# Second norm by halves, convolution edge columns from PSUM, weight splits and constants re-spread over the engines

## The chip, the cores and the metric

One core of one Trainium2 chip. The metric is the device time of one execution in microseconds (us), the median of three runs. Engines, by the names of the profile: PE (TensorE matmuls; PEld its weight loads), DVE (VectorE), ACT (ScalarE), POOL (GpSimd), SP (SyncE, which issues nearly all DMAs).

## The reference

x is (2, 512, 256): two sequences of 512 tokens. xn is its layernorm over the last axis. The output is x + attn(xn) + ffn(xn).

```
y    = gelu(xn @ w_y + b_y)
xb   = xn @ w_x + b_x
conv = conv_b + sum over k of conv_w[k] * xp[:, k:k+T]     # 4 taps, xp is xb with 3 zeros ahead
gx, ga = sigmoid(conv @ w_ig + b_ig), sigmoid(conv @ w_ag + b_ag)
a    = exp(-8 * ga * softplus(a_param));  h = scan of a, gx * conv * sqrt(1 - a*a)
attn = (h * y) @ w_out + b_out
ffn  = (silu(xn @ q(w1).T) * (xn @ q(w3).T)) @ q(w2).T      # q: ternary, threshold mean(|w|) / 2
```

## The kernel before

Tokens lie on partitions for the norm, features for all the rest. A sequence is four tiles of 128 tokens, and 256 features are two chunks. Each engine has one list of instructions in an order written out by hand, and semaphores join the lists; an engine that waits holds up everything behind it in its own list.

Products with the dense weights run in a rounded type. For accuracy each operand is split: `hi` is the rounded copy, `lo` is the value less `hi`. A product is then three terms (hi by hi, w_lo by hi, w_hi by lo), which for one sequence are 12 matmuls of 512 columns.

The order of work around the change, before:

- SP loads four tiles of x of sequence 0 one by one, w_x, the whole of sequence 1 in one DMA (L188), then w_y, w_ig, w_ag, w1, w3, w2, w_out, b_out.
- DVE sets constants, among them two stretches of padding in `gt` (L431, L432), takes statistics (L436, L441) and adds eps (L444); POOL raises the variance to -0.5 (`rstd_of`, L231); DVE normalises (L449). Sequence 0 goes by halves of two tiles, sequence 1 as one piece of four.
- PE transposes xn (L636). ACT rounds the transposed halves from PSUM (`xt_hi_of`, L288); DVE takes the rest (`xt_lo_of`, L455). DVE's list has the statistics of sequence 1, which wait for its load, ahead of `xt_lo_of(0)`.
- PE makes xb of sequence 0 by halves (`first_x_terms`, L740: hi by hi, w_lo by hi, w_hi by lo), then y of sequence 0 (L647), with the transposes of sequence 1 in the middle of it, then xb and y of sequence 1, then the gates, the sum of |w1| and |w3| by a product with ones (L727), and the hidden layer (`hidden`, L664), `down` (L696) and `project` (L706).
- The rounded dense weights `w_hi` of w_x, w_y, w_ig and w_ag are made by ACT (`square_hi`, L283), their `w_lo` by POOL (`square_lo`, L226), each matrix in one instruction.
- The bias b_x passes through the convolution. POOL makes tap constants in `conv_constants` (L233 to L247), the sum of all four in `conv_c` and corrections for the first three columns in `head`. ACT writes the newest tap with that sum (`newest_tap`, L317); DVE adds `head` to the first three columns (L488) and then the three older taps (L492).
- ACT rounds conv (L342) and POOL takes the rest (`lo_of_conv`, L251). DVE makes the ternary w1 and w3 (`ternary_13`, L468, L471).
- ACT loads the table of gelu where gelu first comes (L324). The rounded b_out (`b_split`, L398 on ACT, L272 on POOL) is made before the hidden layer.
- PE begins with 12 matmuls on ones (`warm`, L713), and one more behind each of two waits (L717 to L720).

Of the kernel before, what the change touches and what calls it, by code (L numbers as in the profile page):

```python
# [19 lines left out]
P = 128  # L20
SEQS, SEQ = 2, 512
# [22 lines left out]
def build(nc: bass.Bass, x, dense, w13t, w2t, params, b_out, out):  # L44
# [7 lines left out]
    with ctx:  # L52
# [46 lines left out]
        head = sb("head", [P, TAPS - 1, KC])  # L99
        conv_c = sb("conv_c", [P, 2, KC])  # L100
# [37 lines left out]
        x_loaded = [sem(f"x_loaded{i}") for i in range(TILES + 1)]  # L138
# [13 lines left out]
        b_tap_set, head_set, conv_c_set = sem("b_tap_set"), sem("head_set"), sem("conv_c_set")  # L152
# [28 lines left out]
        def _(sp):  # L181
# [6 lines left out]
            sp.dma_start(x_sb[:, 1], x_dram[1]).then_inc(x_loaded[TILES], 16)  # L188
# [24 lines left out]
        def _(pool):  # L213
# [10 lines left out]
            def square_lo(m):  # L224
                pool.wait_ge(w_hi_set, m + 1)
                nc.gpsimd.tensor_tensor(w_lo[:, m], w_raw[:, m], w_hi[:, m].bitcast(f32), ALU.subtract).then_inc(w_lo_set, 1)  # L226
# [6 lines left out]
            def conv_constants():  # L233

                b_x = par[:, B_X:B_X + KC]
                pool.wait_ge(par_loaded, 16)
                for k in range(TAPS):
                    nc.gpsimd.tensor_tensor(b_tap[:, k], par[:, CONV_W + KC * k:CONV_W + KC * (k + 1)], b_x, ALU.mult).then_inc(b_tap_set, 1)
                pool.wait_ge(b_tap_set, TAPS)
                nc.gpsimd.tensor_scalar(head[:, TAPS - 2], b_tap[:, 0], -1.0, None, ALU.mult).then_inc(head_set, 1)  # L240
                nc.gpsimd.tensor_tensor(conv_c[:, 0], b_tap[:, TAPS - 1], par[:, CONV_B:CONV_B + KC], ALU.add).then_inc(conv_c_set, 1)
                for k in range(1, TAPS - 1):
                    pool.wait_ge(head_set, k)
                    nc.gpsimd.tensor_tensor(head[:, TAPS - 2 - k], head[:, TAPS - 1 - k], b_tap[:, k], ALU.subtract).then_inc(head_set, 1)
                pool.wait_ge(head_set, TAPS - 1)
                pool.wait_ge(conv_c_set, 1)
                nc.gpsimd.tensor_tensor(conv_c[:, 1], conv_c[:, 0], head[:, 0], ALU.subtract).then_inc(conv_c_set, 1)  # L247
# [20 lines left out]
            for s in range(SEQS):  # L268
                for c in range(KC):
                    lo_of_conv(s, c)  # L270
            pool.wait_ge(b_hi_set, 1)
            nc.gpsimd.tensor_tensor(b_split[:, 1], b_row[:, :], b_split[:, 0].bitcast(f32), ALU.subtract).then_inc(b_split_set, 1)  # L272
            for n in range(2 * FULL):
                lo_of_g(n)


        @block.scalar
        def _(act):
# [32 lines left out]
            def newest_tap(s):  # L311

                act.wait_ge(conv_c_set, 2)
                act.wait_ge(xb_psum, s + 1)
                k = TAPS - 1
                for c in range(KC):
                    nc.scalar.activation(conv[:, s, c], slot[X_SLOT[s]][:, c], ACT.Identity,  # L317
                                         scale=par[:, CONV_W + KC * k + c:CONV_W + KC * k + c + 1],
                                         bias=conv_c[:, 1, c:c + 1]).then_inc(tap_set, 1)
# [38 lines left out]
            def decays(s):  # L358

                act.wait_ge(rate_set, 2)  # L360
# [12 lines left out]
            xt_hi_of(0)  # L373
            square_hi(WY)
            newest_tap(0)
            square_hi(WIG)
# [3 lines left out]
            square_hi(WAG)  # L380
            conv_hi_of(0, 0)
            act.wait_ge(w3_loaded, 16)
            abs_sum_of(w13_raw[:, :, W3_AT:W13], KC, junk_b, 1, abs13_set)
            newest_tap(1)
# [12 lines left out]
            act.wait_ge(b_out_loaded, 16)  # L397
            nc.scalar.activation(b_split[:, 0], b_row[:, :], ACT.Copy).then_inc(b_hi_set, 1)  # L398
# [3 lines left out]
            act.wait_ge(w_lo_set, WIG + 1)  # L402
# [25 lines left out]
        def _(dve):  # L428
            nc.vector.memset(quarter[:, :], 0.25).then_inc(quarter_set, 1)
            nc.vector.memset(mult[:, :, :, 0:1], 0.5).then_inc(mult0_set, 1)  # L430
            nc.vector.memset(gt[32:HALF].bitcast(f32), 1.0).then_inc(gt_pads_set, 1)  # L431
            nc.vector.memset(gt[96:P].bitcast(f32), 0.0).then_inc(gt_pads_set, 1)  # L432
# [5 lines left out]
            def variance(s, tiles):  # L438
# [43 lines left out]

            def older_taps(s, c):

                dve.wait_ge(tap_set, KC * s + c + 1)
                dve.wait_ge(head_set, TAPS - 1)
                step = (TAPS - 1) * (KC * s + c)
                nc.vector.tensor_tensor(conv[:, s, c, 0:TAPS - 1], conv[:, s, c, 0:TAPS - 1], head[:, :, c], ALU.add).then_inc(tap_step, 1)  # L488
# [100 lines left out]
            dve.wait_ge(sp_log, 1)  # L589
            nc.vector.scalar_tensor_tensor(out=sp_e[:, 1], in0=par[:, A_PARAM:A_PARAM + KC], scalar=0.0, in1=sp_e[:, 2],  # L590
                                           op0=ALU.max, op1=ALU.add).then_inc(rate_set, 1)
            dve.wait_ge(rate_set, 1)
            nc.vector.tensor_scalar(a_rate[:, :], sp_e[:, 1], -4.0, None, ALU.mult).then_inc(rate_set, 1)
            older_taps(0, 0)
            xt_lo_of(1)
            older_taps(0, 1)
            older_taps(1, 0)
            older_taps(1, 1)
# [31 lines left out]
        def _(pe):  # L630
            def transposes(s):

                for t in range(TILES):
# [7 lines left out]
            def dense_terms(dst, m, terms, first, last, chunk_ready=None):  # L641
                for c in range(KC):
# [68 lines left out]
            def warm(count):  # L711
                for _ in range(count):
                    nc.tensor.matmul(slot[WARM_SLOT][:, 0, 0:P], ones[:, :], ones[:, :], start=True, stop=True)  # L713

            pe.wait_ge(ones_set, 1)
            warm(WARM)
            pe.wait_ge(mv_set, TILES)  # L717
            warm(1)
            pe.wait_ge(rstd_set, 1)
            warm(1)  # L720
            pe.wait_ge(ident_set, 1)
            transposes(0)
# [11 lines left out]
            def first_x_terms(weights, part, ready):  # L734
                for h in range(2):
                    pe.wait_ge(ready, h + 1)
                    for c in range(KC):
                        for o in range(KC):
                            for w in weights:
                                mm = nc.tensor.matmul(slot[X_SLOT[0]][:, o, halves[h]], w[:, WX, c, o * P:(o + 1) * P],  # L740
                                                      part[:, 0, c, halves[h]],
                                                      start=(part is xt_hi and h == 0 and c == 0 and w is w_hi),
                                                      stop=(part is xt_lo and c == KC - 1), skip_group_check=True)
# [12 lines left out]
            dense_terms(slot[Y_SLOT[0]], WY, [(w_hi, xt_lo[:, 0])], False, True).then_inc(y_psum, 1)  # L756
# [14 lines left out]
            def gate_product(s, m, slots, done, between=None):  # L771
                pe.wait_ge(w_lo_set, m + 1)
# [6 lines left out]
            pe.wait_ge(w_lo_set, WAG + 1)  # L779
# [65 lines left out]
```

## Time and profile before

| | us |
|---|---|
| runs (3) | 75.23, 75.66, 76.0: median 75.66 |
| the profiled execution, its own time | 75.99 |
| its span, first to last instruction | 74.2 |
| PE busy | 69.2 (93%) |
| DVE, ACT, POOL busy | 61.2, 48.3, 31.5 |

Times in the trace are counted from the span's start. A row of the timeline is a start, a length, the engine, the line of the code, the operation, what it writes and reads, its shape and a count; the length of a row with a count above one runs from the first start to the last end. Idle time just before a row, and what ended it, stands in square brackets.

### The profile page before, as it was taken

The numbers are of one execution on the slowest core, as the hardware profiler recorded it, in microseconds if no ns is written. First come the engines' busy times: TensorE is split into PE (matmuls) and PEld (weight loads), VectorE is DVE, ScalarE is ACT, GpSimd is POOL, SyncE is SP. The second block draws the span as 40 slices with busy tenths as digits, with TensorE's granted clock in tenths as the row PEclk, the third lists the DMA queues.
The fourth block names the chain that finished last, engine by engine and source line by source line (L and its number), as shares of the span: only waits on it lengthen the run. The fifth ranks groups of instructions, "written<-read, shape, count | busy, mean of one in ns | idle before, by whom it ended". The sixth has DMA issues, their size and how long they took to land.

```text
span 74.2 us, 1064 instructions
## 1 busy us (share of the span) xinstructions
PE 69.2 (93%) x364; PEld 58.6 (79%) x364; DVE 61.2 (82%) x101; ACT 48.3 (65%) x75; POOL 31.5 (43%) x43
## 2 busy tenths in 40 slices
PE   4999969999999999999999999999999999999920
PEld 4985758877888888888888888888899999988800
DVE  4897499999999999999979974697960799999750
ACT  3674523899999999999998978466699910000000
POOL 6385647245851680016002979947689000000000
PEclk9999999999999999999999999999999999999999
DMA  0889999920000000000000000000000000000195
GB/s 8 236 289 333 368 379 342 379 97 9 0 0 0 4 0 0 0 0 0 4 1 0 0 9 0 0 0 0 0 0 0 0 0 0 9 0 0 61 322 183
DMA packets 5095, 5.63 MB, mean 76 GB/s; under 512 B 525, under 2 KB 4578, under 8 KB 5090
## 3 DMA queue, kind: packets, MB, share of 16 engines
q1 hardware_dynamic: 4946, 5.55, 22.1%
q8 instruction: 3, 0.05, 0.3%
q10 hardware_dynamic: 144, 0.01, 0.1%
q14 instruction: 2, 0.02, 0.1%
HBM read 4.51 MB, written 1.05 MB: 75 GB/s over the span
## 4 chain that ended last, share of the span: by engine, by line
PE 80%; DMA 7%; DVE 5%; SPq 3%; issue 1%; DVEq 0%
PE slot L664 25%; PE slot L647 23%; PE slot L696 14%; PE slot L706 8%; DMA x_sb<-x 7%; PE slot L767 4%; PE slot L673 2%; SPq L186 2%; DVE stats L436 2%; PE slot L740 2%; DVE x_sb L551 1%; PE slot L636 1%; DVE xt_lo L455 1%; SPq L183 1%; DVEq L52 0%
## 5 line engine op out<-in xcount | busy, mean ns | idle before, releaser
L256 POOL TENSOR_TENSOR g_lo<-w_raw,g_hi 128x512 fp32r<-128x512 f32 x10 | 14.1, 1421 | 9.0 <-ACT g_hi L338 8.9
L664 PE MATMUL slot<-xt_hi,w_q 128*128 128x512 f32 x40 | 15.7, 393 | 0.0
L664 PE MATMUL slot<-xt_lo,w_q 128*128 128x512 f32 x40 | 15.7, 393 | 0.0
L514 DVE SCALAR_TENSOR_TENSOR w_raw<-w_raw,s,slot 128x512 f32<-128x512 f32 x10 | 7.3, 747 | 3.1 <-ACT w_raw L332 3.0
L696 PE MATMUL slot<-w_q,g_hi 128*128 128x256 f32 x40 | 9.7, 283 | 0.0
L696 PE MATMUL slot<-w_q,g_lo 128*128 128x256 f32 x40 | 9.7, 283 | 0.0
L492 DVE SCALAR_TENSOR_TENSOR conv<-slot,par,conv 128x511 f32<-128x511 f32 (+2 forms) x12 | 9.0, 748 | 0.4
L664 PEld LDWEIGHTS slot<-xt_hi,w_q 128*128 128x128 f32 x40 | 7.5, 188 | 1.7
L664 PEld LDWEIGHTS slot<-xt_lo,w_q 128*128 128x128 f32 x40 | 7.5, 188 | 1.7
L332 ACT ACTIVATE w_raw<-slot,scale 128x512 f32<-128x512 f32 x10 | 6.6, 684 | 3.1 <-PE slot L664 3.1
L696 PEld LDWEIGHTS slot<-w_q,g_lo 128*128 128x128 f32 x40 | 7.7, 192 | 0.0
L696 PEld LDWEIGHTS slot<-w_q,g_hi 128*128 128x128 f32 x40 | 7.7, 192 | 0.0
L226 POOL TENSOR_TENSOR w_lo<-w_raw,w_hi 128x512 fp32r<-128x512 f32 x4 | 5.2, 1295 | 4.5 <-ACT w_hi L283 3.7
L706 PE MATMUL slot<-w_raw,tx 128*128 128x256 f32 x32 | 7.1, 379 | 0.0
L338 ACT ACTIVATE g_hi<-w_raw 128x512 fp32r<-128x512 f32 x10 | 6.3, 629 | 1.1 <-DVE w_raw L514 0.9
L251 POOL TENSOR_TENSOR conv_lo<-conv,conv_hi 128x512 fp32r<-128x512 f32 x4 | 5.4, 1354 | 3.3 <-ACT conv_hi L342 3.3
L706 PEld LDWEIGHTS slot<-w_raw,tx 128*128 128x128 f32 x32 | 6.0, 190 | 0.8
L713 PE MATMUL slot<-ones 128*128 128x128 f32 x28 | 5.3, 357 | 1.0 <-POOL ones L214 1.0
L713 PEld LDWEIGHTS slot<-ones 128*128 128x128 f32 x28 | 4.8, 261 | 1.4 <-POOL ones L214 1.0
L533 DVE TENSOR_TENSOR tx<-tx,mult 128x512 f32<-128x512 f32 x4 | 2.7, 685 | 2.8 <-ACT mult L370 2.8
L538 DVE TENSOR_TENSOR_SCAN tx<-ta,tx 128x512 f32<-128x512 f32 x4 | 4.9, 1224 | 0.1
L647 PE MATMUL slot<-conv_hi,w_hi 128*128 128x512 f32 x12 | 4.7, 395 | 0.0
(111 smaller groups left out, 144.5 us busy)
## 6 DMA issues: line engine op xcount, KB each, us to landing
w_raw<-w13t SPq DMA_DIRECT2D x2, 682.0 KB, 7.6
w_raw<-dense SPq DMA_DIRECT2D x5, 256.0 KB, 5.6
out<-x_sb SPq DMA_DIRECT2D x3, 256.0 KB, 2.2
w_raw<-w2t SPq DMA_DIRECT2D x1, 640.0 KB
x_sb<-x SPq DMA_DIRECT2D x4, 128.0 KB, 2.3
x_sb<-x SPq DMA_DIRECT2D x1, 512.0 KB, 5.3
out<-x_sb SPq DMA_DIRECT2D x2, 128.0 KB, 2.1
w_raw<-w2t SPq DMA_DIRECT2D x2, 42.0 KB
```

The lines of the kernel that those rows point to most:

```text
L226: nc.gpsimd.tensor_tensor(w_lo[:, m], w_raw[:, m], w_hi[:, m].bitcast(f32), ALU.subtract).then_inc(w_lo_set, 1)
L251: nc.gpsimd.tensor_tensor(conv_lo[:, s, c], conv[:, s, c], conv_hi[:, s, c].bitcast(f32), ALU.subtract).then_inc(conv_lo_set, 1)
L256: nc.gpsimd.tensor_tensor(g_lo[:, j, s], g[:, n % RING], g_hi[:, j, s].bitcast(f32), ALU.subtract).then_inc(g_lo_set, 1)
L332: nc.scalar.activation(silu[:, n % RING], slot[H_SLOT[s][j]][:, 0], ACT.Silu, scale=scale[:, 0:1]).then_inc(silu_set, 1)
L338: nc.scalar.activation(g_hi[:, j, s], g[:, n % RING], ACT.Copy).then_inc(g_hi_set, 1)
L492: nc.vector.scalar_tensor_tensor(out=conv[:, s, c, i:], in0=slot[X_SLOT[s]][:, c, 0:SEQ - i], scalar=par[:, CONV_W + KC * k + c:CONV_W + K ...
L514: nc.vector.scalar_tensor_tensor(out=g[:, n % RING], in0=silu[:, n % RING], scalar=s32[:, 0:1], in1=slot[H_SLOT[s][j]][:, 1], op0=ALU.mult ...
L647: mm = nc.tensor.matmul(dst[:, o], w[:, m, c, o * P:(o + 1) * P], v[:, c], start=(first and i == 0 and c == 0), stop=(last and i == len(te ...
L664: mm = nc.tensor.matmul(slot[H_SLOT[s][j]][:, o], w13_q[:, c, col:col + P], v[:, s, c], start=(c == 0 and v is xt_hi), stop=(c == KC - 1 a ...
L696: nc.tensor.matmul(out_tile(s, i, t), v[:, s, rows], w2_q[:, j], start=(j == 0 and t == tiles.start and k == 0), stop=False, skip_group_ch ...
L706: mm = nc.tensor.matmul(out_tile(s, i, t), tx[:, s, c, t * P:(t + 1) * P], w_raw[:, WOUT, c], start=False, stop=(c == KC - 1), skip_group_ ...
L713: nc.tensor.matmul(slot[WARM_SLOT][:, 0, 0:P], ones[:, :], ones[:, :], start=True, stop=True)
```

## The change

- Sequence 1 is loaded by two DMAs and goes through statistics and norm by halves. `xt_lo_of(0)` comes ahead of its statistics.
- Adding eps moves from DVE to POOL, in `rstd_of`. `tap_sum(1..3)` come behind the two `rstd_of` of sequence 0.
- PE: in xb of sequence 0 the lo term of the first half comes ahead of the second half's hi term, and the w_lo terms come third. In y of sequence 0 the w_lo term comes last, behind the transposes of sequence 1, and by chunks. Two single `warm` matmuls go; one of 64 columns comes between the halves of the first transposes.
- `head` goes: `conv_c[k]` is the sum of the first k + 1 constants, ACT writes columns 3 and up, and DVE writes columns 0 to 2 from PSUM (`first_columns`), for the first chunk of sequence 0 between the two halves of the second norm.
- POOL: `w_lo` of w_y waits until all of xn is made and is done in two chunks; `w_hi` of w_ig and w_ag move from ACT to POOL; the decay rates and the padding of `gt` move from DVE to POOL, between the four `lo_of_conv`; `b_split` moves (on ACT and POOL) behind the fifth hidden block.
- ACT: one gelu of one column, on a zero that DVE sets, comes ahead of `square_hi(WY)`, so that gelu's table is loaded there. `gate_x(0)` comes ahead of `conv_hi_of(1, 1)`, the sum of |w3| ahead of `conv_hi_of(0, 0)`.

```diff
             square(WX)
-            sp.dma_start(x_sb[:, 1], x_dram[1]).then_inc(x_loaded[TILES], 16)
+            for i in range(2):
+                t = slice(i * TILES // 2, (i + 1) * TILES // 2)
+                sp.dma_start(x_sb[:, 1, t], x_dram[1][:, t]).then_inc(x_loaded[TILES + i], 16)
...
+            def square_hi(m):
+                pool.wait_ge(w_loaded[m], 16)
+                nc.gpsimd.tensor_copy(w_hi[:, m], w_raw[:, m]).then_inc(w_hi_set, 1)
...
             def rstd_of(s, tiles, ready):
+                pool.wait_ge(mv_set, TILES * s + tiles.stop)
+                nc.gpsimd.tensor_scalar(v_eps[:, s, tiles], mv[:, s, tiles, 1], EPS, None, ALU.add).then_inc(v_set, 1)
                 pool.wait_ge(v_set, ready)
...
-            conv_constants()
-            nc.gpsimd.tensor_scalar(half_b[:, :], par[:, B_IG:B_IG + 2 * KC], 0.5, None, ALU.mult).then_inc(half_b_set, 1)
+            tap_biases()
+            tap_sum(0)
             rstd_of(0, slice(0, TILES // 2), 1)
             rstd_of(0, slice(TILES // 2, TILES), 2)
+            for i in range(1, TAPS):
+                tap_sum(i)
             pool.wait_ge(xn_set, TILES)
             square_lo(WX)
-            rstd_of(1, slice(0, TILES), 3)
-            square_lo(WY)
-            square_lo(WIG)
-            square_lo(WAG)
...
+            rstd_of(1, slice(0, TILES // 2), 3)
+            rstd_of(1, slice(TILES // 2, TILES), 4)
+            pool.wait_ge(xn_set, 2 * TILES)
+            for c in range(KC):
+                square_lo(WY, range(c, c + 1))
+            for m in (WIG, WAG):
+                square_hi(m)
+                square_lo(m)
+            lo_of_conv(0, 0)
+            half_biases()
+            rates()
+            lo_of_conv(0, 1)
+            gt_pads(slice(32, HALF), 1.0, KC)
...
+            lo_of_conv(1, 0)
+            gt_pads(slice(96, P), 0.0, KC + 1)
...
+            lo_of_conv(1, 1)
...
             xt_hi_of(0)
+            act.wait_ge(quarter_set, 2)
+            nc.scalar.activation(gelu_in[:, 1:2], gelu_in[:, 0:1], ACT.Gelu)
             square_hi(WY)
             newest_tap(0)
-            square_hi(WIG)
             xt_hi_of(1)
...
+            def first_columns(s, c):
...
+                nc.vector.scalar_tensor_tensor(
+                    out=conv[:, s, c, 0:k], in0=slot[X_SLOT[s]][:, c, 0:k],
+                    scalar=par[:, CONV_W + KC * k + c:CONV_W + KC * k + c + 1],
+                    in1=conv_c[:, 0:k, c], op0=ALU.mult, op1=ALU.add).then_inc(tap_step, 1)
...
-            dve.wait_ge(x_loaded[TILES], 16)
-            statistics(1, range(TILES))
-            variance(1, range(TILES))
             xt_lo_of(0)
-            normalise(1, range(TILES), 3)
...
+            for i in range(2):
+                dve.wait_ge(x_loaded[TILES + i], 16)
+                statistics(1, tile_halves[i])
+                variance(1, tile_halves[i])
+            normalise(1, tile_halves[0], 3)
+            first_columns(0, 0)
+            normalise(1, tile_halves[1], 4)
             older_taps(0, 0)
             xt_lo_of(1)
...
-            first_x_terms((w_hi,), xt_hi, xt_hi_set)
-            pe.wait_ge(w_lo_set, WX + 1)
-            first_x_terms((w_lo,), xt_hi, xt_hi_set)
-            first_x_terms((w_hi,), xt_lo, xt_lo_set).then_inc(xb_psum, 1)
+            first_x_terms((w_hi,), xt_hi, xt_hi_set, 0)
+            first_x_terms((w_hi,), xt_lo, xt_lo_set, 0)
+            first_x_terms((w_hi,), xt_hi, xt_hi_set, 1)
+            pe.wait_ge(w_lo_set, KC * (WX + 1))
+            for h in range(2):
+                first_x_terms((w_lo,), xt_hi, xt_hi_set, h)
+            first_x_terms((w_hi,), xt_lo, xt_lo_set, 1).then_inc(xb_psum, 1)
             pe.wait_ge(w_hi_set, WY + 1)
-            dense_terms(slot[Y_SLOT[0]], WY, [(w_hi, xt_hi[:, 0])], True, False)
-            pe.wait_ge(w_lo_set, WY + 1)
-            dense_terms(slot[Y_SLOT[0]], WY, [(w_lo, xt_hi[:, 0])], False, False)
-            transposes(1)
-            dense_terms(slot[Y_SLOT[0]], WY, [(w_hi, xt_lo[:, 0])], False, True).then_inc(y_psum, 1)
+            dense_terms(slot[Y_SLOT[0]], WY, [(w_hi, xt_hi[:, 0]), (w_hi, xt_lo[:, 0])], True, False)
+            transposes(1, first_half)
+            transposes(1, second_half)
+            pe.wait_ge(w_lo_set, KC * WY + 1)
+            dense_terms(slot[Y_SLOT[0]], WY, [(w_lo, xt_hi[:, 0])], False, True, chunks=[0])
+            pe.wait_ge(w_lo_set, KC * WY + 2)
+            dense_terms(slot[Y_SLOT[0]], WY, [(w_lo, xt_hi[:, 0])], False, True, chunks=[1]).then_inc(y_psum, 1)
             pe.wait_ge(xt_hi_set, 4)
```

## Rows read from the trace of the kernel before

**Rows 1.** The page: busy time by engine, and the chain that ended last.

```profile
PE 69.2 (93%) x364; PEld 58.6 (79%) x364; DVE 61.2 (82%) x101; ACT 48.3 (65%) x75; POOL 31.5 (43%) x43
...
PE 80%; DMA 7%; DVE 5%; SPq 3%; issue 1%; DVEq 0%
```

**Rows 2.** The chain in order of time: start us, us, what.

```profile
3.04 5.30 DMA x_sb<-x
...
70.17 1.02 DVE x_sb L551 x2
```

**Rows 3.** Timeline of PE, 10.9 to 33.1 us.

```profile
10.90 1.34 PE L740 MATMUL slot<-xt_lo,w_hi 128*128 128x256 f32 x8 [0.63 <-DVE xt_lo L455]
...
13.91 1.04 PE L636 MATMUL slot<-ident,xn_y 128*128 128x128 f32 x8
...
15.71 0.47 PE L647 MATMUL slot<-xt_hi,w_hi 128*128 128x512 f32 x1
16.02 0.39 PE L647 MATMUL slot<-xt_hi,w_lo 128*128 128x512 f32 x1
...
17.68 1.20 PE L647 MATMUL slot<-xt_lo,w_hi 128*128 128x512 f32 x4
...
33.05 0.39 PE L664 MATMUL slot<-xt_hi,w_q 128*128 128x512 f32 x1
```

**Rows 4.** Timeline of DVE, 3 to 32 us.

```profile
3.28 0.75 DVE L436 BATCH_NORM_STATS2 stats<-x_sb 128x6 f32<-128x256 f32 x2
...
5.02 0.30 DVE L441 BATCH_NORM_AGGREGATE mv<-stats 128x2 f32<-128x6 f32 x2
...
5.86 1.54 DVE L449 TENSOR_SCALAR xn_y<-x_sb,mv,rstd 128x256 f32<-128x256 f32 x4 [0.34 <-POOL rstd L231]
...
10.17 1.28 DVE L455 TENSOR_TENSOR xt_lo<-slot,xt_hi 128x512 fp32r<-128x512 f32 x2
...
11.38 1.37 DVE L449 TENSOR_SCALAR xn_y<-x_sb,mv,rstd 128x256 f32<-128x256 f32 x1
...
13.91 0.16 DVE L488 TENSOR_TENSOR conv<-conv,head 128x3 f32<-128x3 f32 x1
14.11 2.32 DVE L492 SCALAR_TENSOR_TENSOR conv<-slot,par,conv 128x511 f32<-128x511 f32 x3
...
25.11 3.16 DVE L468 TENSOR_SCALAR below<-w_raw,thr 128x1408 bf16<-128x1408 f32 x2
28.19 3.22 DVE L471 SCALAR_TENSOR_TENSOR w_q<-w_raw,thr,below 128x1408 fp32r<-128x1408 f32 x2
```

**Rows 5.** Timeline of POOL.

```profile
0.86 0.20 POOL L215 MEMSET ident<- 128x128 f32 x1
...
1.07 0.31 POOL L217 MEMSET w_raw<- 128x256 f32 x1
...
4.91 0.22 POOL L259 TENSOR_SCALAR half_b<-par 128x4 f32<-128x4 f32 x1
5.09 1.53 POOL L231 TENSOR_TENSOR rstd<-v_eps,power 128x2 f32<-128x2 f32 x2
...
11.31 1.29 POOL L226 TENSOR_TENSOR w_lo<-w_raw,w_hi 128x512 fp32r<-128x512 f32 x1
...
33.09 1.45 POOL L272 TENSOR_TENSOR b_split<-b_row,b_split 1x256 fp32r<-1x256 f32 x1 [5.55 <-ACT b_split L398]
...
49.31 1.29 POOL L256 TENSOR_TENSOR g_lo<-w_raw,g_hi 128x512 fp32r<-128x512 f32 x1 [1.16 <-ACT g_hi L338]
```

**Rows 6.** Timeline of ACT, 7 to 24 us.

```profile
7.93 0.60 ACT L288 ACTIVATE xt_hi<-slot 128x512 fp32r<-128x512 f32 x1 [0.21 <-PE slot L636]
...
9.08 0.63 ACT L283 ACTIVATE w_hi<-w_raw 128x512 fp32r<-128x512 f32 x1 [0.55 <-DMA w_raw<-dense]
...
21.19 1.28 ACT L324 ACT_TABLE_LOAD   x1
22.48 1.27 ACT L324 ACTIVATE xn_y<-slot,par 128x512 f32<-128x512 f32 x2
```

More of the change, by code:

```diff
@@ L98, in build @@
         b_tap = sb("b_tap", [P, TAPS, KC])
-        head = sb("head", [P, TAPS - 1, KC])
-        conv_c = sb("conv_c", [P, 2, KC])
+        conv_c = sb("conv_c", [P, TAPS, KC])
+        gelu_in = sb("gelu_in", [P, 2])
         abs_sum = sb("abs_sum", [P, 4])
@@ L135, in xt_bank @@
             return slot[T_SLOT[s]][:, h].rearrange("p (c n) -> p c n", c=KC)
-        x_loaded = [sem(f"x_loaded{i}") for i in range(TILES + 1)]
+        x_loaded = [sem(f"x_loaded{i}") for i in range(TILES + 2)]
         w_loaded = [sem(f"w_loaded{m}") for m in range(5)]
@@ L316, in newest_tap @@
                 for c in range(KC):
-                    nc.scalar.activation(conv[:, s, c], slot[X_SLOT[s]][:, c], ACT.Identity,
+                    nc.scalar.activation(conv[:, s, c, k:], slot[X_SLOT[s]][:, c, k:], ACT.Identity,
                                          scale=par[:, CONV_W + KC * k + c:CONV_W + KC * k + c + 1],
-                                         bias=conv_c[:, 1, c:c + 1]).then_inc(tap_set, 1)
+                                         bias=conv_c[:, k, c:c + 1]).then_inc(tap_set, 1)
             def gelu_of(s):
@@ L416, in _ @@
             g_hi_of(4)
+            act.wait_ge(b_out_loaded, 16)
+            nc.scalar.activation(b_split[:, 0], b_row[:, :], ACT.Copy).then_inc(b_hi_set, 1)
             for n in range(FULL, 2 * FULL):
@@ L583, in _ @@
                 normalise(0, tile_halves[i], i + 1)
-            dve.wait_ge(x_loaded[TILES], 16)
-            statistics(1, range(TILES))
-            variance(1, range(TILES))
             xt_lo_of(0)
-            normalise(1, range(TILES), 3)
[L589 to L593, printed above, removed]
+            for i in range(2):
[5 more added lines that the diff above has]
+            normalise(1, tile_halves[1], 4)
             older_taps(0, 0)
             xt_lo_of(1)
+            first_columns(0, 1)
             older_taps(0, 1)
-            older_taps(1, 0)
-            older_taps(1, 1)
+            for c in range(KC):
+                first_columns(1, c)
+                older_taps(1, c)
             threshold_13()
@@ L630, in _, with transposes @@
         def _(pe):
-            def transposes(s):
-                for t in range(TILES):
+            def transposes(s, tiles):
+                for t in tiles:
                     pe.wait_ge(xn_set, TILES * s + t + 1)
@@ L639, in transposes, with dense_terms @@
                         mm.then_inc(xt_psum, 1)
-            def dense_terms(dst, m, terms, first, last, chunk_ready=None):
-                for c in range(KC):
+            def dense_terms(dst, m, terms, first, last, chunk_ready=None, chunks=range(KC)):
+                for c in chunks:
                     if chunk_ready:
@@ L709, in project, with warm @@
                             mm.then_inc(o_psum, 1)
-            def warm(count):
+            def warm(count, cols):
                 for _ in range(count):
-                    nc.tensor.matmul(slot[WARM_SLOT][:, 0, 0:P], ones[:, :], ones[:, :], start=True, stop=True)
+                    nc.tensor.matmul(slot[WARM_SLOT][:, 0, 0:cols], ones[:, :], ones[:, 0:cols], start=True, stop=True)
+            first_half, second_half = range(0, TILES // 2), range(TILES // 2, TILES)
             pe.wait_ge(ones_set, 1)
[L716 to L720, printed above, removed]
+            warm(WARM, P)
             pe.wait_ge(ident_set, 1)
-            transposes(0)
+            transposes(0, first_half)
+            warm(1, P // 2)
+            transposes(0, second_half)
             def sums_of_w13():
@@ L732, in sum_of_w2, with first_x_terms @@
                 nc.tensor.matmul(sum2, ones[:, :], abs_sum[:, 2:4], start=True, stop=True).then_inc(sum2_psum, 1)
[L734 to L743, printed above, removed]
+            def first_x_terms(weights, part, ready, h):
+                pe.wait_ge(ready, h + 1)
+                for c in range(KC):
+                    for o in range(KC):
+                        for w in weights:
+                            mm = nc.tensor.matmul(slot[X_SLOT[0]][:, o, halves[h]], w[:, WX, c, o * P:(o + 1) * P],
+                                                  part[:, 0, c, halves[h]],
+                                                  start=(part is xt_hi and h == 0 and c == 0 and w is w_hi),
+                                                  stop=(part is xt_lo and h == 1 and c == KC - 1), skip_group_check=True)
```

76 lines of the change are left out of this document (39 added, 37 removed).

## The prediction

> **What bounds the kernel now.** I read the page's busy times first: PE is busy for 69.2 of 74.2 us, and the chain that ended last is PE for 80% [rows 1]. So the next question is where PE is not at full pace, and the chain in order of time answers it: PE carries the chain from 10.90 to 70.17, where the last output begins [rows 2, 3]. Behind that point nothing can be won but by fewer or faster matmuls, and the change takes away none there. Ahead of it stands the load of sequence 1 (3.04 to 8.35) [rows 2], and PE idles 0.63 us until the first `xt_lo` of sequence 0 [rows 3]. The timelines of DVE, POOL and ACT then show why it was late: DVE's list puts the statistics of sequence 1 ahead of it, so `xt_lo` began at 10.17 [rows 4] though its `xt_hi` was done at 8.53 [rows 6].
>
> PE's pace is the yardstick for all that follows. From 15.71 (xb of sequence 1) to 33.05 (hidden layer) it does 72 matmuls of 512 columns and two small sums in 17.34 us [rows 3], which is 0.237 each if the two sums together count as one more. There are restarts in it: the first matmul behind a wait holds its successor off 0.31 us instead of 0.23 [rows 3]. I ask when PE reaches xb of sequence 1, and carry the gain from there to the end, wait by wait.
>
> **The change, step by step.**
>
> *First norm.* Statistics of tiles 2 and 3 ended with the second pair of aggregates at 5.32 [rows 4]; one eps instruction of some 0.1 us leaves DVE ahead of them, so 5.2. POOL now adds eps (0.22, as its row of that kind [rows 5]) and raises to the power (1.53 for two, so about 0.8 [rows 5]): 5.2 + 0.1 + 0.25 + 0.8 = 6.4. Two normalisations at 0.4 each, overlapping a little (1.54 for four [rows 4]), end at 7.15, against 7.40. The first half gains more (POOL came to it only at 5.09, behind ten small constants [rows 5]), but the second half sets what follows.
>
> *`xt_lo` of sequence 0.* In the kernel before, `xt_hi` of the second half was done at 8.53, that is 1.13 us behind the last xn [rows 4, 6]. 7.15 + 1.13 = 8.28, and one `xt_lo` (1.28 for two that overlap, so 0.68) gives 9.02 instead of 11.45. PE's xb of sequence 0 then ends near 10.3 instead of 12.1: by 9.0 it has done the first half's hi and lo terms and the second's hi term, has eight w_lo matmuls under way to about 9.9, and four lo matmuls remain.
>
> *Gelu's table.* A load takes 1.28 us [rows 6]. From 8.2, when ACT is done with `xt_hi`, load, gelu of one column (0.2 as a small operation) and `square_hi(WY)` (0.63) end at 10.33. Before, w_y landed at 9.08 [rows 6]. So `square_hi(WY)` is 0.6 late, but PE is ready for it only at 10.3: the cost is 0.1, and even that is covered, since the next thing PE needs comes later still. Nothing is won at the old place either: gelu's results were not what PE waited for.
>
> *Second norm: here the time is set.* DVE is free at 8.94, behind `xt_lo`; the first half of x has to be there by then, the second by 9.8. The whole landed at 8.35 before [rows 2], and the split costs SP one issue more, about 0.45 us. Four statistics at 0.33 and two pairs of aggregates (a pair of both kinds takes 0.97 [rows 4]) end at 10.75. The first half's aggregates are there at 9.9; POOL's eps and power take it to 11.0; the second half's, queued behind, to 12.0. Two normalisations end at 12.8, against 13.72: before, the first of the four took 1.37 us [rows 4] because it met POOL's `w_lo` of w_y (11.31 to 12.60 [rows 5]). A normalisation can be held up by POOL, then, and the first half's pair now starts just as POOL's power of the second half runs. The rows say that a power does not do it: in the first norm the second power (up to 6.62 [rows 5]) ran beside normalisations that took 1.54 for four [rows 4]. I take no loss.
>
> The Trainium skill speaks against the change here (SBUF — State Buffer, Who interferes with whom): a DVE instruction of this mode and any POOL instruction exclude each other for its whole length, whichever begins first. The trace agrees for the subtraction (1.37 for 0.4 [rows 4]) and not for the power. By the rule the first pair would wait for 12.0 instead of 11.1, xn would end at 13.5, and the gain would be 0.35.
>
> `first_columns` (0.16, as the `head` add that it replaces [rows 4]) lies in DVE's wait from 11.8 to 12.0 and costs nothing; without that cover it would cost 0.2.
>
> *w_lo of w_y.* It now waits for the last xn: 12.85, and half of 1.29 with its start is 0.68 [rows 5], so 13.55 and 14.2. PE has done eight hi matmuls of y by 12.3 and eight transposes (0.11 each [rows 3]) by 13.1, waits 0.45, does two matmuls, waits 0.2, does two more, and comes to xb of sequence 1 at 14.75 to 14.9, since two restarts cost 0.1 each. Before: 15.71. **Gain 0.8 to 0.95.**
>
> *From there to the hidden layer.* The restarts at 15.71 and 17.68 go away if `xt_hi` and `xt_lo` of sequence 1 are early: `xt_hi` is done at 14.1, and `xt_lo`, behind older taps of 2.32 us [rows 4] from 12.7, at 16.2, needed at 16.6. The eight matmuls from 15.71 took 1.97 [rows 3] where 1.85 is the pace: **0.1 to 0.2 more.**
>
> POOL's new work is the one unknown. `w_hi` of two matrices comes to it, an operation that the trace shows on no POOL row. Below it stands a bare write: memsets of 128 and 256 columns took 0.20 and 0.31 [rows 5], so 512 would take 0.52. Above it stands the subtraction with two reads, 1.29 [rows 5]. I take 0.9, in the middle, as it has one read. From 14.2: twice (0.9 + 1.29 + waits of 0.1) is 18.75, `lo_of_conv(0, 0)` 20.05, one bias and three rates at 0.25 21.0, `lo_of_conv(0, 1)` 22.3. PE needs this last one at about 22.7 (14.85, 24 matmuls of sequence 1, 8 of the gate, 2 more). Spare: 0.4. At 0.52 it is 1.2; at 1.29 PE waits 0.4.
>
> *Off the path.* Padding on POOL is two memsets of about 0.95 each (0.31 and six times 0.107); they lie between `lo_of_conv`s that PE needs at 27.5, with a us to spare. ACT's two `square_hi` leave it, and `b_split` (0.4 on ACT, 1.45 on POOL [rows 5]) moves into a place where POOL idled 1.16 before its next `g_lo` [rows 5]; its DMA is needed only at the end of `down`. The ternary w1 and w3 ended at 31.41 [rows 4], 1.6 ahead of PE. DVE ends its taps near 23.6, 1.3 earlier than before, so they should end by 30.1 at the old pace, still 1.8 ahead of PE's 31.95; of that the two memsets, now beside the two compares (3.16 [rows 4], with two `lo_of_conv` beside them), could take 1.9 if they held them up fully, so this cover is thin but enough to within 0.1.
>
> **The sum.** 0.85 + 0.2 = 1.05 us. The output and the scan shift with the hidden layer, as no wait between is touched. The profiled execution took 75.99; it becomes 74.9. The median of the runs stands 0.33 below that, so it goes from 75.66 to **74.6**.
>
> **Rivals.**
>
> *The second norm is late (within 1%).* The chain through POOL's two powers and the second half of x decides. If the second half lands at 10.4 instead of under 9.8, or the first pair of normalisations is held behind the second power (0.7 late), 0.6 to 0.7 goes one to one: gain 0.4, 75.3. For it: the one load took 5.30 us [rows 2], and every later load is issued later. Against: 1.4 us of slack on the landing, and the first norm's four at full pace beside a power. The rule of the Trainium skill above is this rival's second condition.
>
> *POOL's list becomes the bound (slower).* Place: `lo_of_conv(0, 1)`, for which PE waits in the first gate. Both copies count, so lateness is twice (copy less 0.9) less the spare 0.4, and the gain is gone at a copy of about 1.6; at 2.2 PE waits 2.2 us and the time is 75.66 - 1.05 + 2.2 = 76.8. For it: POOL's power took 0.8 us for two columns [rows 5], so columns alone don't price an operation there. Against: a subtraction with twice the reads took 1.29.
>
> *The table load costs more in its new place (within 1%).* If it also held ACT back for as long again, about 1.35 us, `square_hi(WY)` would end at 11.7, y of sequence 0 would end near 15.5, and the gain falls to 0.4: 75.3. Against: gelu began 0.01 us behind the load's end [rows 6]. The Trainium skill (ScalarE: Activation LUTs, What ACT_TABLE_LOAD costs) gives a load with its drain as 2.66 us; the trace shows 1.28 alone.
>
> That the table is not kept, and loaded again at the first real gelu, costs the forecast nothing, as the load was not on the path at either place.
>
> **How the numbers follow.** Within 1% (0.76 us) of 75.66 is about what a measurement can tell from no change. The forecast (gain 0.8 to 1.5, the upper end if PE's wait for w_lo of w_y is missing) has 0.72, all of it faster by over 1%. The late second norm has 0.17 and the load's drain 0.03: 0.20 within 1%. POOL's list has 0.08, slower. The range goes from 73.9 (gain 1.5, and 0.25 for a lower draw of the runs) to 75.7: it takes in the second rival and a copy of 1.29, and leaves out the slow copy.
>
> **What would show it.** Right: `xt_lo` of sequence 0 ends near 9.0; normalisations of the second norm at 0.4 each, the last one near 12.8; PE idle 0.4 and 0.2 ahead of the two chunks of w_lo, xb of sequence 1 at 14.8, no idle of PE in the gates, hidden layer at 32.0, span 73.1. Wrong: PE idle ahead of the first gate's lo term (POOL), `square_hi(WY)` ending behind 10.5 (table), statistics of sequence 1 waiting for a load behind 9.0 (DMA).

## The result, and the profile after

The change made the kernel slower: 75.88 us (median of 20 runs, 75.45 to 76.22) against 75.41 (20 runs of the kernel before beside them, 74.89 to 76.6). The ratio is 1.0066, with an interval from 1.0043 to 1.009, which is 0.3 to 0.7 us; the forecast was 74.6. Ratios and intervals, here and below, leave out the slow executions that some kernels had (the slowest, 237.25 us, was the profiled one of `d1_w_lo_early`), so they differ a little from the quotients of the medians, which are of all runs. The profiled execution took 75.86 with a span of 74.0. The page answers to [rows 1]:

```profile
PE 68.6 (93%) x362; PEld 58.7 (79%) x362; DVE 59.0 (80%) x95; ACT 47.7 (64%) x74; POOL 37.4 (51%) x55
...
PE 65%; POOL 12%; DVE 7%; issue 5%; DMA 3%; ACT 2%; DVEq 0%; POOLq 0%
```

PE has only 65% of the chain, against 80%. The chain in order of time [rows 2] tells where it left PE:

```profile
13.79 9.68 PE slot L689 x40
...
37.81 5.55 PE slot L706 x24
...
43.39 0.69 ACT w_raw L371
44.07 0.53 ACT g_hi L377
...
44.67 2.55 POOL g_lo L281 x2
47.22 0.61 DVE gt_hi L608
...
48.49 1.23 DVE gt L609
...
50.24 0.76 DVE w_raw L556
...
51.05 2.11 PE slot L706 x8
```

Before, PE carried the chain from 10.90 to the last output. Now it leaves PE at 43.36, in the middle of the hidden layer, goes through ACT, POOL and two casts of DVE, and is back on PE at 51.05. The timeline of PE, which answers to [rows 3], has both halves of the story:

```profile
10.53 0.50 PE L689 MATMUL slot<-xt_hi,w_hi 128*128 128x512 f32 x1
...
13.79 1.42 PE L689 MATMUL slot<-xt_hi,w_lo 128*128 128x512 f32 x4 [0.27 <-POOL w_lo L233]
15.05 0.40 PE L689 MATMUL slot<-xt_hi,w_hi 128*128 128x512 f32 x1
...
32.11 0.39 PE L706 MATMUL slot<-xt_hi,w_q 128*128 128x512 f32 x1
...
50.34 0.39 PE L706 MATMUL slot<-xt_lo,w_q 128*128 128x512 f32 x1
51.05 0.50 PE L706 MATMUL slot<-xt_hi,w_q 128*128 128x512 f32 x1 [0.31 <-DVE w_raw L556]
```

The front half did what was forecast: the hidden layer begins at 32.11 instead of 33.05 [rows 3]. Its tenth full block of eight matmuls, at 51.05, follows the matmul before it by 0.71 where the pace is 0.23: 0.48 is lost there. DVE and POOL show the same stretch; first DVE, which answers to [rows 4] in its first two lines (the others have no row there):

```profile
11.17 0.73 DVE L484 TENSOR_SCALAR xn_y<-x_sb,mv,rstd 128x256 f32<-128x256 f32 x2 [0.28 <-POOL rstd L249]
12.18 0.74 DVE L484 TENSOR_SCALAR xn_y<-x_sb,mv,rstd 128x256 f32<-128x256 f32 x2
...
47.21 1.24 DVE L608 CAST gt_hi<-w_raw 42x1024 fp32r<-42x1024 f32 x1
48.49 1.72 DVE L609 CAST gt<-w_raw 42x1024 fp32r<-42x1024 f32 x1
50.24 1.41 DVE L556 SCALAR_TENSOR_TENSOR w_raw<-w_raw,s,slot 128x512 f32<-128x512 f32 x2
...
57.73 0.69 DVE L575 TENSOR_TENSOR tx<-tx,mult 128x512 f32<-128x512 f32 x1 [2.83 <-ACT mult L409]
```

Then POOL, which answers to [rows 5]:

```profile
11.41 0.73 POOL L249 TENSOR_TENSOR rstd<-v_eps,power 128x2 f32<-128x2 f32 x1
13.00 1.43 POOL L233 TENSOR_TENSOR w_lo<-w_raw,w_hi 128x256 fp32r<-128x256 f32 x2 [0.86 <-DVE xn_y L484]
14.38 0.61 POOL L228 CAST w_hi<-w_raw 128x512 fp32r<-128x512 f32 x1
...
47.17 0.73 POOL L313 TENSOR_TENSOR b_split<-b_row,b_split 1x256 fp32r<-1x256 f32 x1
48.37 1.30 POOL L281 TENSOR_TENSOR g_lo<-w_raw,g_hi 128x512 fp32r<-128x512 f32 x1 [0.47 <-ACT g_hi L377]
```

And the same two casts in the timeline of DVE of the kernel before:

```profile
47.85 0.85 DVE L566 CAST gt_hi<-w_raw 42x1024 fp32r<-42x1024 f32 x1
48.74 0.69 DVE L567 CAST gt<-w_raw 42x1024 fp32r<-42x1024 f32 x1
49.46 0.75 DVE L514 SCALAR_TENSOR_TENSOR w_raw<-w_raw,s,slot 128x512 f32<-128x512 f32 x1
```

A cast takes 0.69. After the change `b_split` on POOL (47.17 to 47.90) began 0.04 ahead of the first cast, which ended 0.55 behind it, at 48.45. So the second cast started late, at 48.49, when the next `g_lo` had begun (48.37 to 49.67); it ended 0.55 behind that, at 50.21. Two casts of 0.69 became 1.24 and 1.72. The product g behind them, for which PE's tenth block waits, came at 50.24, where before it came at 49.46 although the hidden layer had begun 0.94 later.

My theory from here: the whole loss is `b_split` in its new place, by way of the two casts. The rivals: the loss lies elsewhere in the change and the casts only show it; and, for the front half, that the gain is not of the size that one profile shows.

### The profile page after: what moved, and what is told of

It is laid out like the page before. It is cut to its first block, busy times and chain, and to the rows that moved or that the text cites. A ratio compares the mean times of both kernels' runs of the same rounds, so it can differ in the third digit from the quotient of the medians.

```text
span 74.0 us, 1074 instructions
## 1 busy us (share of the span) xinstructions
PE 68.6 (93%) x362; PEld 58.7 (79%) x362; DVE 59.0 (80%) x95; ACT 47.7 (64%) x74; POOL 37.4 (51%) x55
## 3 DMA queue, kind: packets, MB, share of 16 engines
HBM read 4.51 MB, written 1.05 MB: 75 GB/s over the span
## 4 chain that ended last, share of the span: by engine, by line
PE 65%; POOL 12%; DVE 7%; issue 5%; DMA 3%; ACT 2%; DVEq 0%; POOLq 0%
PE slot L689 21%; PE slot L706 15%; PE slot L738 14%; PE slot L748 8%; PE slot L812 4%; POOL rstd L249 4%; POOL g_lo L281 3%; DMA par<-params 3%; POOL w_lo L233 3%; PE slot L715 2%; DVE xn_y L484 2%; DVE gt L609 2%; POOL v_eps L246 1%; DVE x_sb L593 1%; DVE w_raw L556 1%
## 5 line engine op out<-in xcount | busy, mean ns | idle before, releaser
L281 POOL TENSOR_TENSOR g_lo<-w_raw,g_hi 128x512 fp32r<-128x512 f32 x10 | 14.7, 1490 | 14.4 <-ACT g_hi L377 14.4
L755 PE MATMUL slot<-ones 128*128 128x128 f32 (+1 forms) x26 | 5.3, 388 | 1.0 <-POOL ones L216 1.0
L233 POOL TENSOR_TENSOR w_lo<-w_raw,w_hi 128x512 fp32r<-128x512 f32 (+1 forms) x5 | 5.3, 1075 | 1.2 <-DVE xn_y L484 0.9
L474 DVE BATCH_NORM_STATS2 stats<-x_sb 128x6 f32<-128x256 f32 x8 | 3.1, 417 | 2.3 <-DMA x_sb<-x 2.3
```

Of the source, the lines that this page charges most:

```text
L233: nc.gpsimd.tensor_tensor(w_lo[:, m, c], w_raw[:, m, c], w_hi[:, m, c].bitcast(f32), ALU.subtract).then_inc(w_lo_set, len(chunks))
L281: nc.gpsimd.tensor_tensor(g_lo[:, j, s], g[:, n % RING], g_hi[:, j, s].bitcast(f32), ALU.subtract).then_inc(g_lo_set, 1)
L755: nc.tensor.matmul(slot[WARM_SLOT][:, 0, 0:cols], ones[:, :], ones[:, 0:cols], start=True, stop=True)
```

## The experiments

**1. `b_split` alone, in three places.** `a1_split_back` is the kernel after with `b_split` at its old place:

```diff
+            pool.wait_ge(b_hi_set, 1)
+            nc.gpsimd.tensor_tensor(b_split[:, 1], ...)
...
-                if n == FULL - 1:
-                    pool.wait_ge(b_hi_set, 1)
-                    nc.gpsimd.tensor_tensor(b_split[:, 1], ...)
```

(and the same for ACT's half of it).

> The changed kernel with b_split at its old place on ACT and POOL. Theory (POOL's b_split and the g_lo behind it hold up DVE's two casts of the tail, g(6) comes 0.9 late, and PE waits 0.47 and a restart of 0.1 ahead of the tenth hidden block): that wait goes, 75.3 us, ratio to before 0.998. Rival 1 (only ACT's 0.3 us for b_split counts, as it delays silu of block 5): 75.3 as well. Rival 2 (the loss sits in the first 32 us, in the work moved to POOL): 75.9, ratio 1.006.

`a2_split_two_later` leaves ACT's half in its new place and moves POOL's alone, behind two more `g_lo`:

```diff
-                if n == FULL - 1:
+                if n == FULL + 1:
```

> The changed kernel with POOL's half of b_split two g_lo later, ACT's half where the change put it. Theory: the casts meet no POOL instruction that began just before them, g(6) starts by 49 and PE does not wait: 75.3, ratio 0.998, as with both halves back. Rival 1 (ACT's 0.3 us): 75.9, PE still waits 0.4 or more ahead of the tenth block. Rival 2: 75.9 without such a wait.

`b1_split_moved` is the kernel before with only this move, on ACT and POOL.

> The kernel before with nothing but b_split moved to where the change has it, on ACT and POOL. Theory: the two casts take 1.2 and 1.7 us instead of 0.86 and 0.69, PE waits 0.3 to 0.6 ahead of the tenth hidden block: 75.8 to 76.0, ratio 1.005 to 1.008. Rival 2 (the loss sits in the first 32 us): 75.4, ratio 1.00.

Measured, against the kernel before on the same chip (75.55): `a1_split_back` 75.11, ratio 0.993 [0.9901, 0.9959]; `a2_split_two_later` 75.13, 0.9939 [0.991, 0.9968]; `b1_split_moved` 76.29, 1.0104 [1.0064, 1.0144]. The loss goes when POOL's half alone goes elsewhere, and comes by the move alone. DVE in `a1_split_back`:

```profile
46.93 1.03 DVE L607 CAST gt_hi<-w_raw 42x1024 fp32r<-42x1024 f32 x1
47.98 0.69 DVE L608 CAST gt<-w_raw 42x1024 fp32r<-42x1024 f32 x1
```

Beside them POOL's `g_lo`, the third of three and the next:

```profile
43.59 3.81 POOL L281 TENSOR_TENSOR g_lo<-w_raw,g_hi 128x512 fp32r<-128x512 f32 x3 [0.43 <-ACT g_hi L376]
48.34 1.48 POOL L281 TENSOR_TENSOR g_lo<-w_raw,g_hi 128x512 fp32r<-128x512 f32 x1 [0.95 <-ACT g_hi L376]
```

In `a2_split_two_later`, DVE and then POOL:

```profile
47.47 0.69 DVE L608 CAST gt_hi<-w_raw 42x1024 fp32r<-42x1024 f32 x1
48.20 0.69 DVE L609 CAST gt<-w_raw 42x1024 fp32r<-42x1024 f32 x1
...
48.63 1.41 POOL L281 TENSOR_TENSOR g_lo<-w_raw,g_hi 128x512 fp32r<-128x512 f32 x1 [1.15 <-ACT g_hi L377]
```

In `b1_split_moved`, with POOL's `b_split` and PE's wait below them:

```profile
47.91 1.26 DVE L567 CAST gt_hi<-w_raw 42x1024 fp32r<-42x1024 f32 x1
49.20 1.70 DVE L568 CAST gt<-w_raw 42x1024 fp32r<-42x1024 f32 x1
...
47.88 0.74 POOL L275 TENSOR_TENSOR b_split<-b_row,b_split 1x256 fp32r<-1x256 f32 x1
...
51.74 0.50 PE L665 MATMUL slot<-xt_hi,w_q 128*128 128x512 f32 x1 [0.31 <-DVE w_raw L515]
```

The same arithmetic gives the end of every cast that was held: POOL's end and 0.55. In `b1_split_moved` `b_split` ended at 48.62 and the cast at 49.17. In `a1_split_back` and in the kernel before the first cast was held too, by the third of the `g_lo` ahead of it (1.03 and 0.85 instead of 0.69), but the second found POOL idle. Where the cast came first, POOL was held: in `a2_split_two_later` the second cast began at 48.20 and the `g_lo` of 48.63 beside it took 1.41 instead of 1.29. It ended 1.15 behind the cast, and so did the `g_lo` of 48.34 in `a1_split_back`. On either side the one that was held thus ended its length alone less 0.14 behind the other (0.69 and 0.55, 1.29 and 1.15).

The Trainium skill has this rule (SBUF — State Buffer, Who interferes with whom): a DVE instruction in a mode that takes both port pairs and one of POOL shut each other out for the whole length, and whichever was issued first keeps the ports. The traces agree for these casts, from both sides. They do not agree for the power beside the normalisations (below).

How 0.75 comes of it, between the traces of `a1_split_back` (span 73.23) and of the kernel after (73.98): PE's tenth block costs 0.48 and its restart 0.1, which puts the end of PE's work at 69.76 instead of 69.18. The rest, 0.17, lies behind the last addition of the output. DVE's scan chain began at 57.73 instead of 56.91, 0.82 later, which is more than PE lost. So the five additions came in one piece (to 71.14), without the wait for PE that stands between them in `a1_split_back` (to 70.56), and the span ended 2.84 behind them instead of 2.67. It was 2.87 and 2.95 in the two other kernels where they came in one piece (`b1_split_moved`, `e1_g6_first`), and 2.68 and 2.69 in two where they did not (the kernel before, `a2_split_two_later`). The output's DMAs of 256 KB took 2.3 to 2.4 us to land (median) in the kernel after and these two, and 2.2 in the three others, which fits DMAs issued closer together; that this is the reason is argued only. The medians of the two kernels differ by 0.77, though they were not measured side by side.

**2. Is it the tenth block's wait, or the casts themselves?** `e1_g6_first` is the kernel after, with `b_split` left in its new place, and DVE's product `g_of(6)`, for which PE's tenth block waits, put ahead of the casts:

```diff
             g_of(5)
+            g_of(6)
             tail_hi()
-            g_of(6)
```

> The changed kernel, b_split left where the change put it, with DVE's product g(6) ahead of the two casts of the tail. Theory (the casts are still held up by POOL, but no longer stand ahead of the product that PE waits for): no wait of PE ahead of the tenth block, 75.1 to 75.2. Rival (what is held up is something else of the hidden stage, ACT or POOL's g_lo): 75.7 or more.

It was a miss: 76.46 against 75.47, 1.0122 [1.0077, 1.0168], in the rival's range but not for the rival's reason. PE did reach the tenth block without a wait, at 50.68, and the casts were held again. DVE and PE tell where the delay went:

```profile
48.69 1.62 DVE L608 CAST gt_hi<-w_raw 42x1024 fp32r<-42x1024 f32 x1
50.34 1.82 DVE L609 CAST gt<-w_raw 42x1024 fp32r<-42x1024 f32 x1
...
58.47 0.69 DVE L575 TENSOR_TENSOR tx<-tx,mult 128x512 f32<-128x512 f32 x1 [2.83 <-ACT mult L409]
...
69.24 1.99 PE L748 MATMUL slot<-w_raw,tx 128*128 128x256 f32 x8 [0.60 <-DVE tx L586]
```

Behind the later product the first cast met a whole `g_lo` (48.47 to 49.76) and the second the next one (50.32 to 51.62). All later products were late, hence ACT's `g_hi`, its table and `mult`, hence the scan: it began at 58.47, 1.56 behind `a1_split_back`. In `a1_split_back` PE's last product could have stood a scan 0.36 later (its last `tx` ended at 67.63, the four matmuls behind it take 1.15, and PE was done at 69.18). 1.56 less 0.36 is 1.2, and PE's last product did end 1.2 later, at 70.39. So the time that DVE loses counts in two places, at the tenth block and through the scan; which of them ends last depends on the order. Moving the product ahead did not help; moving `b_split` away from the casts did.

**3. The front half: what ties the kernel before, and what in the change unties it.** `before_again` is the kernel before, unchanged, for its scatter.

> The kernel before, unchanged, for a second profile of it. Its profiled execution took 75.99 us, 0.6 over the median of its 20 runs (75.41), which lie between 74.89 and 76.60, where those of the changed kernel lie between 75.45 and 76.22. Theory: the profile of before caught an execution in which the load of sequence 1 landed late (8.35 us); in a typical one it lands near 7 and the second norm ends up to 0.6 earlier, so this profile should show a span near 73.6 and statistics of sequence 1 starting before 8. Rival: the spread comes from elsewhere, and the statistics start at 8.3 to 8.4 again with another span. Ratio 1.00 in both.

75.83 against 75.55, 1.002 [0.9987, 1.0052]. It caught another late execution (75.81, span 74.0): the statistics began at 8.20, neither before 8 (theory) nor at 8.3 to 8.4 (rival). Its trace, DVE and PE:

```profile
8.20 1.41 DVE L436 BATCH_NORM_STATS2 stats<-x_sb 128x6 f32<-128x256 f32 x4 [0.77 <-DMA x_sb<-x]
...
32.87 0.39 PE L664 MATMUL slot<-xt_hi,w_q 128*128 128x512 f32 x1
```

Three traces have the chain of [rows 2] from this load. Statistics begin at 8.37, 8.20 and (in `b1_split_moved`) 8.10; the hidden layer at 33.05, 32.87 and 32.81: 24.68, 24.67 and 24.71 later. In these three, 0.27 apart, the kernel before moves one to one with the landing of that load. Its 20 runs scatter over 1.7 us (74.89 to 76.6), the 20 of the kernel after beside them over 0.77, and 12 of `a1_split_back` over 0.58 (74.84 to 75.42). That the landing makes all of this scatter fits, but is not shown: no early execution was profiled.

`c1_one_load` is `a1_split_back` with sequence 1 in one DMA again (and DVE's waits to match):

```diff
-            for i in range(2):
-                t = slice(i * TILES // 2, (i + 1) * TILES // 2)
-                sp.dma_start(x_sb[:, 1, t], ...).then_inc(x_loaded[TILES + i], 16)
+            sp.dma_start(x_sb[:, 1], x_dram[1]).then_inc(x_loaded[TILES], 16)
```

> The changed kernel with b_split back and sequence 1 in one load again, its statistics by halves as in the change. Theory (in the changed order nothing waits for this load before 9.0, so that the time no longer follows its landing): 75.1, with statistics of sequence 1 starting at 9.0 to 9.1 though the load lands at 8.0 to 8.4. Rival (the two loads are part of the gain): 75.4 or more.

75.18 against 75.47, 0.9976 [0.9945, 1.0007]: by the times alone not clear of no change, so the reading rests on the trace. Its load was issued at 3.06 and took 5.3, so it landed as late as the profiled one before, and yet:

```profile
9.07 0.74 DVE L471 BATCH_NORM_STATS2 stats<-x_sb 128x6 f32<-128x256 f32 x2
...
32.14 0.39 PE L703 MATMUL slot<-xt_hi,w_q 128*128 128x512 f32 x1
```

The statistics did not wait, and the hidden layer began within 0.05 of `a1_split_back` (32.09). It is not the split of the load that unties the changed kernel: DVE is at `xt_lo_of(0)` until then.

`b2_x1_first` (the kernel before, with the load of sequence 1 issued ahead of w_x) and `b3_xt_lo_first` (the kernel before, with only `xt_lo_of(0)` moved ahead) try the two parts alone:

```diff
+            sp.dma_start(x_sb[:, 1], x_dram[1]).then_inc(x_loaded[TILES], 16)
             square(WX)
-            sp.dma_start(x_sb[:, 1], x_dram[1]).then_inc(x_loaded[TILES], 16)
```

> The kernel before with one line moved: the load of sequence 1 is issued ahead of that of w_x. Theory (before is bound by the landing of this load, which three profiles show at 8.35, 8.17 and 8.08 us and whose scatter is the scatter of its times): statistics of sequence 1 start near 7.4, the hidden layer near 32.2 instead of 32.8 to 33.05, the median is 75.0 to 75.2 (0.4 under before) and the runs scatter less. Rival (the gain of the front is that of the reordered lists, and the load is hidden): 75.5 and the same scatter.

75.79 against 75.87, 1.0017 [0.9978, 1.0057]: w_x was now late in its turn (its rounding on ACT began at 8.41, and PE waited until 9.67). No gain and a scatter of 1.28 is what the rival said, but with another load as the tie this run decides nothing.

> The kernel before with DVE's xt_lo of sequence 0 ahead of the statistics of sequence 1, and no other part of the change. PE's wait of 0.5 to 0.9 us ahead of the xt_lo matmuls should go. Theory (what sets the hidden layer's start is the end of the second norm, and this order alone puts it 0.6 later, because xt_lo of the second half ends at 9.1): no gain, 75.4 to 76.0, PE waits further on instead, for w_lo of w_y or the transposes. Rival (that PE wait was the loss, as the chain shows): 75.0.

77.84 against 75.87, 1.0297 [1.0248, 1.0346]. POOL took both `w_lo` ahead of the last norm, on top of DVE's four normalisations, and PE waited for them:

```profile
12.22 3.31 DVE L449 TENSOR_SCALAR xn_y<-x_sb,mv,rstd 128x256 f32<-128x256 f32 x4 [1.12 <-POOL rstd L231]
...
13.48 1.20 PE L647 MATMUL slot<-xt_hi,w_lo 128*128 128x512 f32 x4 [1.25 <-POOL w_lo L226]
```

3.31 for what takes 1.54 alone [rows 4], and 2.34 in the kernel before: the order by itself costs 2 us. In the change POOL waits with `w_lo` of w_y until xn is made (it begins at 13.00, behind a wait for xn of 0.86), and the normalisations take 0.41 each.

**4. The table of gelu.** `c2_table_late` is `a1_split_back` without the early gelu, so that the table is loaded at the first real one.

> The changed kernel with b_split at its old place and without the early gelu, so that gelu's table is loaded where gelu first comes, near 20 us. Theory (neither place is on the path): 75.1, as with the early load, to within 0.15; the rounded w_y is made 0.9 us earlier and PE does not start y earlier for it. Rival (the early load is part of the gain): 75.4 or more. Rival 2 (it costs in its new place, as it delays the rounded w_y): 75.0 or less.

75.2 against 75.87, 0.9953 [0.9919, 0.9986], within 0.1 of `a1_split_back`, and the hidden layer at 32.15: the place of the load is worth nothing that these runs can show.

**5. A version better than both.** In `d1_w_lo_early`, `a1_split_back` with `square_hi(WY)` ahead of the early gelu, POOL does the first chunk of `w_lo` of w_y before the second norm, and PE takes its two matmuls ahead of the transposes of sequence 1:

```diff
             square_lo(WX)
+            square_lo(WY, range(0, 1))
...
+            dense_terms(slot[Y_SLOT[0]], WY, [(w_lo, xt_hi[:, 0])], False, True, chunks=[0])
             transposes(1, first_half)
             transposes(1, second_half)
```

> A new version: the changed kernel with b_split back, ACT's rounded w_y ahead of the gelu table, and the first chunk of w_lo of w_y in the 1.3 us in which POOL idled ahead of the second norm (8.74 to 10.1), so that PE has it ahead of the transposes of sequence 1. Theory (PE's waits of 0.31 and 0.13 us for w_lo of w_y with a restart of 0.1 each are what is left of the front): hidden layer 0.3 to 0.5 us earlier, 74.7 to 74.9. Rival (POOL's chunk delays the first rstd of sequence 1 by as much, and PE waits for xn or xt_hi instead): 75.1.

> The version with the first chunk of w_lo of w_y in POOL's idle time once more, for a profile of it and a second comparison with the kernel before. As its first 11 undisturbed runs (74.71 to 75.28): 74.9 to 75.0. In its profile: chunk 0 of w_lo at 9.3 to 10.0, the first rstd of sequence 1 at most 0.3 later than 10.13, PE's wait ahead of the transposes under 0.1 and one wait for w_lo (chunk 1) or xt_hi, xb of sequence 1 at 14.7 to 14.9 instead of 15.05.

74.95 against 75.87, 0.9909 [0.9875, 0.9943], and, repeated as `d1_again`, 75.03 against 75.47, 0.9938 [0.9906, 0.997]. The trace is that of the repeat; its PE:

```profile
12.52 0.62 PE L688 MATMUL slot<-xt_hi,w_lo 128*128 128x512 f32 x2
...
13.88 0.73 PE L688 MATMUL slot<-xt_hi,w_lo 128*128 128x512 f32 x2
14.76 0.50 PE L688 MATMUL slot<-xt_hi,w_hi 128*128 128x512 f32 x1
```

Both waits for `w_lo` are gone, and PE comes to xb of sequence 1 at 14.76 instead of 15.02; a new wait of 0.4, for `xt_hi`, stands in their place, as the rival said. Of the 0.26 the hidden layer keeps 0.12 (31.97), where 0.3 to 0.5 was expected. It beats the kernel before by 0.6 to 0.9%, and so by these ratios the kernel after by more, though not side by side with it; from `a1_split_back` its times can't be told apart.

## Why the prediction was wrong, step by step

**The step that failed** is "The output and the scan shift with the hidden layer, as no wait between is touched", and ahead of it that `b_split` "moves into a place where POOL idled 1.16 before its next `g_lo`". I looked for POOL's idle time, and it was there: no `g_lo` came late through it. But I did not look at what DVE does in those 1.16 us. Its two casts lie there, and the row of the first one before (0.85, against 0.69 for its twin) already showed that POOL can hold them. Nor did `b_split` fit by its own row: 1.45 [rows 5] is more than 1.16. That row was itself a hold (it ended 0.59 behind a compare of DVE, 32.94 to 33.95); in the new place `b_split` took 0.73. I weighed the rule of the ports at the second norm and nowhere else; the change puts POOL work beside DVE in a second place. Cost: 0.75 us by the traces, 0.74 in `b1_split_moved` beside `before_again` if the 0.06 by which its hidden layer began earlier is added to the spans' 0.68.

**The second step that failed** is the shift to the median: "it goes from 75.66 to 74.6". The gain of 1.05 was worked out against the profiled execution, and that one (75.99) was a late draw for the very reason that the change removes, the landing of the load. I carried the whole gain over. By the tie above, an execution of 75.5 would have had its hidden layer near 32.55 (0.5 ahead of 33.05), and against that 32.1 is a gain of 0.45. This is worked out and not shown, as no trace of so early an execution is at hand; it agrees with the 0.44 of `a1_split_back` (75.55 to 75.11). So typical gain and loss are 0.45 and 0.75, and the sum is 0.3 slower; 0.47 was measured, with 0.3 at the near end of its interval. What the 0.17 between them is stays open.

**What held.** Against its own execution the front half came out at 0.94 of 1.05:

- First norm done at 7.30 (forecast 7.15), `xt_lo` of sequence 0 at 9.16 (9.02), second norm at 12.92 (12.8). The second half's landing never mattered. (Two sums were off: 8.28 and 0.68 make 8.96, not 9.02, and two pairs of statistics and aggregates of 0.97 from 8.94 end at 10.88, not 10.75, where 10.89 was measured. Neither moves the forecast, since POOL's second power ends later.)
- *The late second norm, and the rule of the ports there.* The first pair of normalisations (11.17) and the second power (11.41) ran side by side, at 0.41 each and 0.73: neither was held, as the row of the first norm had said.
- `w_lo` of w_y: 0.74 and 0.69 a chunk (0.68), PE idle ahead of both chunks, xb of sequence 1 at 15.05 (14.75 to 14.9). From there to the hidden layer 17.06 instead of 17.34: 0.28 (0.1 to 0.2).
- *POOL's list.* The copy, bounded by 0.52 and 1.29 and taken at 0.9, took 0.61; PE had no wait in the gates. This rival is out.
- *The table.* ACT, which answers to [rows 6]:

```profile
8.46 1.28 ACT L414 ACT_TABLE_LOAD   x1
...
9.86 0.61 ACT L322 ACTIVATE w_hi<-w_raw 128x512 fp32r<-128x512 f32 x1
```

It ended at 10.47 (forecast 10.33), and PE began y at 10.53. No further stop of ACT follows the load, so that rival is out as well.

- *The ternary weights* ended at 31.10, not 30.1: the quantising took 4.25 instead of 3.22 [rows 4], with the last `lo_of_conv` beside it (1.79 instead of 1.29). Of POOL's memsets the first (0.94) ended ahead of the compares, and the second (1.58) ran beside them; they took 2.78, less than the 3.16 of before. Of the cover called thin 1.0 was left ahead of PE. The memsets and the eps on POOL were not tried alone.

The slower side had a chance of 0.08, all of it on POOL's list in the gates. The right place was POOL's list again, but 25 us later, and by its ports rather than its order.

## What to carry to other kernels

An engine's idle stretch is a free place for an instruction only if the engine that shares its ports is not busy there with work that can be held: read both timelines for the stretch, not one. A small instruction that starts first can cost its neighbour most of its length, and push the neighbour's next one into the next collision. And when the profiled execution is a late one, ask what made it late: if the change removes just that, the gain over the median is smaller than the gain over the profile.

## What the runs showed of the hardware

- A `b_split` of one row (0.73 on POOL) cost DVE 1.58 over two casts, the second by way of the next `g_lo`: 1.24 and 1.72 instead of 0.69 each. A held cast ended 0.55 behind the POOL instruction in all five kernels read for it (before, after, `a1_split_back`, `b1_split_moved`, `e1_g6_first`).
- The same held the other way and for other pairs: whichever was held ended its length alone less 0.13 to 0.15 behind the other. A `g_lo` of POOL (1.29 alone) ended 1.15 behind a cast; `b_split` (0.73) ended 0.59 to 0.60 behind a compare (before) and a subtraction (`a2_split_two_later`) of DVE; that subtraction (1.22) ended 1.07 to 1.08 behind a `g_lo` (before, `a2_split_two_later`). The held normalisation of [rows 4] does not fit: it ended 0.15 behind `w_lo` and takes 0.41 alone.
- POOL's power of two columns took 0.71 to 0.77, and neither it nor a normalisation beside it was held; the eps beside a normalisation of the first norm took 0.37 instead of 0.22. Its rounding copy of 512 columns (0.61) is nearer to a bare write (0.52, estimated from the memsets) than to a subtraction (1.29).
